# Twelve small VectorE instructions in place of a GpSimd power, and a 16x16 covariance in place of a pass of scores

## The chip, the cores and the metric

The kernel runs on one core of one Trainium2 chip. The core has a matrix engine (TensorE, PE in the profile, PEld its weight loads), a vector engine (VectorE, DVE), an activation engine (ScalarE, ACT), a general engine (GpSimd, POOL) and SyncE (SP), which issues most DMAs. Each engine runs its own instruction stream in order and waits on semaphores. The metric is the device time of one execution in microseconds; lower is better.

## The reference, cut to what matters

Sixteen batches (B = 16) of 512 queries of 256 numbers go through two transformer layers with a context of 1601 keys. In cut form:

```python
# layer 0, attention: 16 heads of 16; q and k are normalised per head
q = layernorm(q, ln_g, ln_b); k = layernorm(k, ln_g, ln_b)     # (x-mu)*rsqrt(var+1e-5)*g+b, over 16
attn = softmax(einsum('bhqd,bhkd->bhqk', q * 4, k)); out = attn @ v
x = x + out @ Wp + bp
x = x + gelu(LN(x) @ U1 @ V1 + b1) @ U2 @ V2 + b2              # layer 0, feed forward
# layer 1, attention: one head of 16 for all, scores normalised over the keys
q = LN(x) @ Wq + bq; k = ctx @ Wk + bk; v = ctx @ Wv + bv
s = einsum('bqd,bkd->bqk', q, k) / 16
s = (s - mean(s, -1)) / (std(s, -1, ddof=1) + 1e-8)
x = x + tile(softmax(s) @ v, 16) @ Wout + bout
# layer 1, feed forward: soft mixture of 64 experts (stage two of the kernel, untouched)
```

## The kernel before

The kernel has two stages with separate memory. Stage two (the experts, some 2230 us) is not touched. Stage one does both attentions and the first feed forward, batch after batch.

**Steps.** For one batch the heavy work of the first attention is cut into 4 groups of 4 heads x 13 chunks of keys = 52 steps. In a step c of a group the PE computes four blocks of scores (L766), which ACT exponentiates (L999), and multiplies the step before's probabilities with the values (L777, four matmuls). Between these stand up to six *row pieces*: scores of 401 keys for the group that comes next (L744), of which DVE takes the row maximum out of PSUM (L1148). The 64 pieces of a group are dealt as 6 in steps 0 to 8, 5 in steps 9 and 10, none in 11 and 12. The pieces go through two PSUM banks in turn, so the PE can be at most two pieces ahead of DVE. At the end of a group the maxima are transposed, split into three bf16 parts (`nT`, L1162 to L1166 on DVE) and written by DMA into a row of the query stack (`qst<-nT`, L532); the first score of the next group waits for it.

**The weave.** All other work is put between these by hand: `woven()` gives each small job a position, a step number with a fraction (thirds: three places in a step). Jobs with `of` = 1 are the *head* of the batch that comes next: load and transpose the context (`T`), keys and values (`K`), queries (`Q`), keys and values of the second attention (`kv1`), and the transposes of normalised heads (`X`). Jobs with -1 are the *tail* of the batch before: `attnT`, `proj`, the norms (`lnv`, `lna`), the feed forward (`xT`, `u1`, `V1`, `gpre`, `gtanh`, `gpost`, `U2`, `v2`) and the second attention (`q1`, `st` ... `out`). Each engine walks the same table and runs its own part of each job; an engine that waits inside a job holds back all that stands behind it. Before batch 0 the head runs alone, and after batch 15 the tail runs alone.

**Norm of heads.** POOL squares (`sq`, L591), DVE sums over 16 (`ssq`, L1142), and POOL in `kn` adds epsilon (L597), raises to the power -0.5 (L598) and multiplies (L600). This comes for five blocks n = 0 to 4 of a batch; block 1 is the queries, block 4 has 65 rows only. The PE's transposes `X` and then POOL's `X` (three instructions that split into bf16 planes, L607 to L609), the stores `stX` and the stack loads `ldS` of SP follow.

**Second attention.** `ldX` (SP) loads x and, by L519, the 32 x 1601 keys and values `kv1T`. `st` n is one of 16 passes of f32 scores, 128 queries x 401 keys (L845), read by DVE with bn_stats (L1211). `stv` joins them, `sgp` on POOL makes 1/(std + 1e-8) from the variance with two powers, `qtr` transposes the queries to tokens, `qs` scales them, `v1` transposes keys and values (L858), `qaT` transposes back, and `s1`, `pv1`, `o1`, `out` make scores, probabilities (ACT, L1044) and the output. The score's mean enters as a 17th row of the queries against a row of ones (`R1` = 65 partitions).

Of the kernel before, what the change touches and what calls it, by code (L numbers as in the profile page):

```python
# [59 lines left out]
def woven():  # L60
# [53 lines left out]
    for f in range(FC):  # L114
        put((10.67, 11.0, 11.34, 11.67, 15.67, 16.67, 17.67, 18.67)[f], -1, "V1", f)
        put((11.01, 11.5, 12.34, 13.0, 16.34, 17.34, 18.34, 19.34)[f], -1, "gpre", f)
        put((12.0, 12.67, 13.67, 14.34, 18.0, 19.0, 20.0, 21.0)[f], -1, "gtanh", f)
        put((12.01, 12.68, 13.68, 14.35, 18.01, 19.01, 20.01, 21.01)[f], -1, "gpost", f)
        put((15.34, 16.34, 17.34, 18.34, 20.0, 21.0, 22.0, 23.0)[f], -1, "U2", f)
# [157 lines left out]
def stage_one(nc, x, ctx_d, mask, w, x3_d, xn_d, xnT_d, ident, psum):  # L277

    with ExitStack() as st:
# [66 lines left out]
        kv1T = sb("kv1T", [R1, NK])  # L346
        v1a = sb("v1a", [P, KC, 2 * A1])
        q1T = sb("q1T", [R1, S])
        qa = sb("qa", [P, QT, R1])
        st1 = sb("st1", [P, QT, 4, 6])  # L350
        mv1 = sb("mv1", [P, QT, 2])
# [1381 lines left out]
```

## Time and profile before

| what | value |
|---|---|
| median of 3 runs | 7277.4 us (7277.04 to 7296.08) |
| the profiled execution | 7297.03 us, its span 7295.2 us |
| mean granted clock of TensorE | 0.952 |
| PE busy | 6573.1 us (90%) |
| PEld, DVE, ACT, POOL busy | 44%, 49%, 44%, 41% |
| head alone, up to the first score of batch 0 | to 258 us |
| 16 batches | last exponential starts at 4890.5 us; batch 10 takes 293.4 us |
| tail alone of the last batch | to 5068 us |
| stage two | to the end |

An engine's busy share is over the whole span. The granted clock is the rate of TensorE that the chip allowed, 1.0 being 2.4 GHz and 0.5 being 1.2 GHz. Step times below are the distances between the first exponentials of steps.

### The profile page before, as it was taken

To read this page: it belongs to the slowest core of one execution; us is meant where nothing else is said; L and a number is where in the kernel's file an instruction comes from. 1 tells how busy PE (TensorE), PEld (TensorE's weight loads), DVE (VectorE), ACT (ScalarE), POOL (GpSimd) and SP (SyncE) were. 2 spreads that over 40 slices of the span, in tenths; PEclk is the share of its full clock that TensorE was granted. 3 is DMA by queue.
4 is the path that set the end of the run, shared out by engine and by line. 5 is a ranking of instruction groups with operands and counts; after the bars stand their busy time and mean duration, and the time that the engine had idled before them with its cause. 6 is when DMAs were issued, how large, how long until landed. Compare 5 with 4: busy or idle time off the path is not lost. (4 is left out here: it accounts for less than half of the span.)

```text
span 7295.2 us, 92018 instructions
## 1 busy us (share of the span) xinstructions
PE 6573.1 (90%) x35805; PEld 3225.4 (44%) x35869; DVE 3609.2 (49%) x7012; ACT 3207.4 (44%) x5697; POOL 2959.5 (41%) x1969
## 2 busy tenths in 40 slices
PE   3789999999989999999999999985899999999999
PEld 1223333333333333333333333222788888766666
DVE  2555555655656556566565565641766666200000
ACT  1355555555555555555555555551322222111111
POOL 5327447365483663844736538223222222100000
PEclk8799999999999999999999999995999999999999
DMA  2341332432323323133242231302344444411111
GB/s 60 67 77 49 65 56 63 72 60 51 63 59 68 67 52 76 44 70 60 60 74 59 55 71 47 57 16 79 104 153 159 156 164 158 156 52 52 52 52 41
DMA packets 364931, 546.03 MB, mean 75 GB/s; under 512 B 59824, under 2 KB 281984, under 8 KB 364240
## 3 DMA queue, kind: packets, MB, share of 16 engines
q1 hardware_dynamic: 321232, 498.18, 28.2%
q10 hardware_dynamic: 43264, 41.95, 1.7%
q8 instruction: 284, 4.65, 0.3%
q14 instruction: 151, 1.24, 0.1%
HBM read 387.94 MB, written 151.28 MB: 74 GB/s over the span
## 5 line engine op out<-in xcount | busy, mean ns | idle before, releaser
L1148 DVE TENSOR_REDUCE mx<-psum 128x1 f32<-128x401 f32 x4096 | 2193.4, 570 | 1722.6 <-PE psum L744 1711.7
L999 ACT ACTIVATE probs<-psum 128x512 f32<-128x512 f32 (+1 forms) x3328 | 1920.1, 597 | 1149.4 <-PE psum L766 1145.8
L744 PE MATMUL psum<-kst,qst 96*128 96x401 bf16 x4096 | 1434.7, 352 | 268.3 <-DVE mx L1148 202.7
L766 PE MATMUL psum<-qst,kst 99*128 99x512 bf16 (+1 forms) x3328 | 1299.7, 394 | 152.1 <-ACT probs L999 116.6
L744 PEld LDWEIGHTS psum<-kst,qst 96*128 96x128 bf16 x4096 | 404.2, 99 | 1553.3 <-DVE mx L1148 1246.0
L777 PE MATMUL psum<-probs,vaug 128*17 128x512 f32 x6656 | 904.5, 616 | 0.0
L598 POOL TENSOR_TENSOR ssq<-ssq,powers 128x64 f32<-128x64 f32 (+1 forms) x80 | 722.2, 9027 | 6.7
L766 PEld LDWEIGHTS psum<-qst,kst 99*128 99x128 bf16 (+1 forms) x3328 | 330.9, 100 | 860.8 <-ACT probs L999 463.0
L1415 POOL TENSOR_TENSOR disp<-disp,rz 128x2048 f32<-128x2048 f32 x64 | 294.9, 4608 | 909.2 <-DVE rz L1634 909.2
L1434 PE MATMUL psum<-phi,xT 128*128 128x128 f32 x4096 | 511.7, 279 | 39.8 <-DMA xT<-xnT_scratch 32.5
L1434 PEld LDWEIGHTS psum<-phi,xT 128*128 128x128 f32 x4096 | 479.9, 193 | 87.4 <-issue 79.8
L1449 PE MATMUL psum<-disp,xnb 128*128 128x128 f32 x4096 | 489.3, 278 | 29.7 <-POOL disp L1415 19.0
L1585 ACT ACTIVATE disp<-psum 128x512 f32<-128x512 f32 x256 | 152.9, 597 | 807.7 <-PE psum L1502 606.2
L1512 PE MATMUL psum<-disp 128*128 128x257 f32 x2048 | 487.1, 381 | 12.3 <-issue 7.2
L1449 PEld LDWEIGHTS psum<-disp,xnb 128*128 128x128 f32 x4096 | 474.3, 194 | 37.9 <-POOL disp L1415 19.6
L1499 PE MATMUL psum<-xT,phi 128*128 128x512 f32 x1024 | 485.4, 596 | 0.2 <-issue 0.2
L1512 PEld LDWEIGHTS psum<-disp 128*128 128x128 f32 x2048 | 388.1, 190 | 143.5 <-issue 93.0
L625 POOL TENSOR_SCALAR rs<-mv 128x4 f32<-128x4 f32 x48 | 11.2, 232 | 1053.5 <-DVE mv L1204 1052.3
L702 PE MATMUL psum<-wkv,cT 128*128 128x512 f32 (+1 forms) x832 | 409.4, 615 | 14.0 <-ACT pl L992 6.3
L1536 ACT ACTIVATE disp<-psum 128x512 f32<-128x512 f32 x256 | 152.1, 597 | 463.1 <-PE psum L1434 463.1
L1687 DVE RECIPROCAL rc<-psum 128x1 f32<-128x1 f32 x64 | 5.8, 153 | 599.9 <-PE psum L1512 599.9
L1641 DVE TENSOR_TENSOR ysb<-psum,be 128x512 f32<-128x512 f32 x128 | 88.5, 692 | 428.9 <-PE psum L1464 428.9
(185 smaller groups left out, 7761.3 us busy)
## 6 DMA issues: line engine op xcount, KB each, us to landing
xnb<-xn_scratch SPq DMA_DIRECT2D x256, 512.0 KB, 3.7
kst<-k_planes SPq DMA_DIRECT2D x384, 200.1 KB, 9.1
k_planes<-pl SPq DMA_DIRECT2D x96, 384.0 KB, 3.2
y_scratch<-ysb ACTq DMA_DIRECT2D x128, 256.0 KB, 3.4
disp<-y_scratch SPq DMA_DIRECT2D x16, 2048.0 KB, 9.4
vaug<-v_scratch SPq DMA_DIRECT2D x64, 442.0 KB, 3.4
v_scratch<-vst SPq DMA_DIRECT2D x48, 544.0 KB, 3.1
cin<-in_ctx SPq DMA_DIRECT2D x48, 512.0 KB, 3.8
```

Source lines behind the costliest of these rows:

```text
L598: link(pool.tensor_tensor(r, r, powers[:, 0:1, None].broadcast_to((P, m, H)), ALU.pow))
L702: last = mm(hb[0:m, :], cT[:, n % 2, k, a * P:a * P + m], wkv[:, k, :], start=(k == 0), stop=(k == 1))
L744: mm(to[:, 0:PW], qst[g][0:NP, j, t * P:(t + 1) * P], kst[g][0:NP, j, k0:k0 + PW], start=True, stop=True).then_inc(m_full, 1)
L766: mm(bank[S_BANK[n % 2]][0:m, :], kst[g][0:NR, j, c * P:c * P + m], qst[g][0:NR, j, :], start=True, stop=True).then_inc(s_full, 1)
L777: last = mm(bank[V_BANK][32 * j:32 * j + HV, :], vaug[0:m, g % 2, c, HV * j:HV * (j + 1)], probs[0:m, 4 * (k % 2) + j, :], start=(c == 0), ...
L999: fn(probs[0:m, 4 * (k % 2) + j, :], bank[S_BANK[j % 2]][0:m, :], ACT.Exp, scale=float(HD) ** 0.5).then_inc(s_exp, 1)
L1148: v.tensor_reduce(mx[:, u // 4, u % 4:u % 4 + 1], bank[M_BANK[r % 2]][:, 0:PW], AX.X, ALU.max).then_inc(m_free, 1)
L1415: pool.tensor_tensor(d, d, rz[:, n % 2, None, :].broadcast_to((P, B, SL)), ALU.mult).then_inc(normed, 1)
L1434: last = mm(bank[u % 4][:, a * SL:(a + 1) * SL], xT[:, 4 * q + a, k, t * P:(t + 1) * P], phi[:, k, s * SL:(s + 1) * SL], start=(k == 0), s ...
L1449: last = mm(bank[4 + n % 2][:, (2 * a + h) * SL:(2 * a + h + 1) * SL], xnb[:, a, t, h * P:(h + 1) * P], disp[:, (QT * s + t) % RING, b, :] ...
L1499: mm(o, phi[:, k, c * P:(c + 1) * P], xT[:, b, k, :], start=(k == 0), stop=False)
L1512: last = mm(bank[4 + t][:, 0:D + 1], ex[n % 4][:, t * P:(t + 1) * P], ya[b % 2][:, e, :], start=(e == 0), stop=(e == NSL - 1))
```

## The change

**Inverse roots.** `kn` on POOL loses the add and the power. In their place `ssq` on DVE, behind its sum, makes the inverse root itself: an add, a shift and a multiply-add on the bits (a first guess from the constant `ROOT_SEED`), and three Newton steps of three instructions, twelve instructions, each waiting for the one before. They stand at 1.3 behind the block's last `K` or `Q` and not at 0.7.

**Variance from a covariance.** The 16 passes `st` and `stv`, `qtr` go. Since the variance of q.k over the keys is q' C q with C the covariance of the keys, DVE centres the keys at the start of the batch (`kc`: a sum over 1601, a scaling, a subtraction), PE transposes keys and values (`v1`, now at 1.67), multiplies keys by keys over 13 chunks (`cov`, 16x16), and DVE scales that (`cove`). Once the queries are there, PE makes C q (`cq`), DVE multiplies by q (`cqe`), PE sums over 16 and transposes (`cs`). With centred keys the row for the mean goes too, so operands shrink from 65 to 16 partitions.

**Places.** `attnT` moves from 3.34 to 4.0, some feed-forward jobs by a third of a step, and all of the second attention behind the queries moves 3 to 4 steps earlier: `s1` stands at 35.0, two a step, where it stood at 38.67, four in two steps; `st3`, the store of the tail, at 49.0 and not 51.67.

```diff
-        put(head[done] + 0.7, 1, "ssq", n)
-        put(head[done] + 0.72, 1, "kn", n)
+        put(head[done] + 1.3, 1, "ssq", n)
+        put(head[done] + 1.32, 1, "kn", n)
...
-    put(3.34, -1, "attnT", 0)
-    put(3.67, -1, "attnT", 1)
-    put(5.0, -1, "proj", 0)
+    put(4.0, -1, "attnT", 0)
+    put(4.34, -1, "attnT", 1)
+    put(5.34, -1, "proj", 0)
...
-    for n in range(16):
-        put(30.0 + n / 3, -1, "st", n)
-    put(35.67, -1, "stv")
-    put(35.7, -1, "sgp")
-    put(36.0, -1, "qtr")
-    put(36.67, -1, "qs")
-    put(37.0, -1, "v1")
-    put(37.34, -1, "qaT")
-    put(37.67, -1, "v1e")
-    put(38.0, -1, "q1a")
+    put(1.0, -1, "kc")
+    put(1.67, -1, "v1")
+    put(2.34, -1, "v1e")
+    put(3.0, -1, "cov")
+    put(3.5, -1, "cove")
+    put(30.0, -1, "cq")
+    put(30.67, -1, "cqe")
+    put(31.34, -1, "cs")
+    put(32.0, -1, "cse")
+    put(32.01, -1, "sgp")
+    put(33.0, -1, "qs")
+    put(33.67, -1, "qaT")
+    put(34.34, -1, "q1a")
     for c in range(KC):
-        put(38.67 + c // 4 * 2 + c % 4 / 3, -1, "s1", c)
+        put(35.0 + 0.5 * c, -1, "s1", c)
     for k in range(4):
-        put((40.34, 42.34, 44.34, 45.34)[k], -1, "pv1", k)
-    put(45.67, -1, "o1")
+        put((36.95, 38.95, 40.95, 41.95)[k], -1, "pv1", k)
+    put(42.34, -1, "o1")
...
-                r = ssq[:, n % 2, 0:m, :]
-                link(pool.tensor_scalar(r, r, HD * EPS, None, ALU.add))
-                link(pool.tensor_tensor(r, r, powers[:, 0:1, None].broadcast_to((P, m, H)), ALU.pow))
+                r = rstd[:, n % 2, 0:m, :]
...
             def heads_transposed(b, h):
                 pe.wait_ge(m_free, RING["out", b * G + G - 1] + 1)
-                if b >= 1:
-                    pe.wait_ge(t_act, at("t_act", b - 1, "xT", 3, h))
+                pe.wait_ge(t_dve, at("t_dve", b, "cove"))
...
+            def covariance(b):
+                pe.wait_ge(t_dve, at("t_dve", b, "v1e"))
+                for c in range(KC):
+                    m = key_rows(c)
+                    last = mm(b6[0:A1, 0:A1], kva[0:m, c, 0:A1], kva[0:m, c, 0:A1], start=(c == 0), stop=(c == KC - 1))
+                last.then_inc(t_mm, 1)
+
+            def covariance_queries(b):
+                pe.wait_ge(t_act, at("t_act", b, "q1"))
+                mm(b7[0:A1, :], cov[:, :], q1T[:, :], start=True, stop=True).then_inc(t_mm, 1)
...
-                v.tensor_reduce(ssq[:, n % 2, 0:m, :], sq[:, 0:m, :].rearrange("p c (h d) -> p c h d", h=H), AX.X,
-                                ALU.add).then_inc(ssq_done, 1)
+                z, y, t = ssq[:, 0:m, :], rstd[:, n % 2, 0:m, :], root[:, 0:m, :]
+                link(v.tensor_reduce(z, sq[:, 0:m, :].rearrange("p c (h d) -> p c h d", h=H), AX.X, ALU.add))
+                link(v.tensor_scalar(z, z, HD * EPS, None, ALU.add))
+                link(v.tensor_scalar(t.bitcast(I32), z.bitcast(I32), 1, None, ALU.logical_shift_right))
+                link(v.tensor_scalar(y.bitcast(I32), t.bitcast(I32), -1, ROOT_SEED, ALU.mult, ALU.add))
+                for i in range(3):
+                    link(v.scalar_tensor_tensor(out=t, in0=y, scalar=-0.5, in1=z, op0=ALU.mult, op1=ALU.mult))
+                    link(v.tensor_tensor(t, t, y, ALU.mult))
+                    ins = v.scalar_tensor_tensor(out=y, in0=t, scalar=1.5, in1=y, op0=ALU.add, op1=ALU.mult)
+                    if i < 2:
+                        link(ins)
+                ins.then_inc(ssq_done, 1)
...
+            def keys_centred(b):
+                dve.wait_ge(kv1_loaded, at("kv1_loaded", b, "ldX"))
+                link(v.tensor_reduce(kmean[:, :], kv1T[0:A1, :], AX.X, ALU.add))
+                link(v.tensor_scalar(kmean[:, :], kmean[:, :], 1.0 / NK, None, ALU.mult))
+                v.tensor_scalar(kv1T[0:A1, :], kv1T[0:A1, :], kmean[:, 0:1], None, ALU.subtract).then_inc(kc_ready, 1)
```

**POOL, block 4 of the head, steps 26 to 28 of the kernel before.** The inverse root of block 3 stands ahead of the squares of block 4, and between these and the root of block 4 stand a norm (`lna` 2) and a bias (`base` 3):

```order
L597 TENSOR_SCALAR ssq<-ssq 128x64
L598 TENSOR_TENSOR ssq<-ssq,powers 128x64
L600 TENSOR_TENSOR kraw<-kraw,ssq 128x1024
L591 TENSOR_TENSOR sq<-kraw 128x256
L625 TENSOR_SCALAR rs<-mv 128x4
L626 TENSOR_TENSOR rs<-rs,powers 128x4
L628 TENSOR_SCALAR xn<-xw,mv,rs 128x256 x4
L618 TENSOR_TENSOR xw<-xw,bor 128x1024
L597 TENSOR_SCALAR ssq<-ssq 128x16
L598 TENSOR_TENSOR ssq<-ssq,powers 128x16
L600 TENSOR_TENSOR kraw<-kraw,ssq 128x256
```

The same place in the changed kernel (the line numbers are its own):

```order
L607 TENSOR_TENSOR kraw<-kraw,rstd 128x1024
L600 TENSOR_TENSOR sq<-kraw 128x256
L632 TENSOR_SCALAR rs<-mv 128x4
L633 TENSOR_TENSOR rs<-rs,powers 128x4
L635 TENSOR_SCALAR xn<-xw,mv,rs 128x256 x4
L625 TENSOR_TENSOR xw<-xw,bor 128x1024
L607 TENSOR_TENSOR kraw<-kraw,rstd 128x256
```

The two powers are gone, and the norm and the bias still stand between the squares and the multiplication, so they run on POOL while DVE makes the root of block 4. In block 1 the three plane instructions of the first `X` stand in that place; in blocks 0, 2 and 3 the squares and the multiplication are neighbours.

**DVE, steps 1 to 3 of the changed kernel.** Before, there is nothing in these rows but maxima, `attn` and the moments of the queries:

```order
L1163 TENSOR_REDUCE mx<-psum 128x1 x7
L1224 TENSOR_REDUCE kmean<-kv1T 16x1
L1225 TENSOR_SCALAR kmean<-kmean 16x1
L1226 TENSOR_SCALAR kv1T<-kv1T,kmean 16x1601
L1163 TENSOR_REDUCE mx<-psum 128x1 x6
L1189 RECIPROCAL rec<-psum 128x16
L1191 TENSOR_TENSOR attn<-psum,rec 128x64 x4
L1138 BN_STATS bst<-cin 128x6 x4
L1141 BN_AGGR mv<-bst 128x2 x4
L1163 TENSOR_REDUCE mx<-psum 128x1 x2
L1252 COPY kva<-psum 128x12x32
L1253 COPY kva<-psum 65x32
```

The centring stands behind the seventh maximum of the batch (six of step 0 and one of step 1), and five maxima of step 1 stand behind it.

**PE, end of step 1 of the changed kernel,** with what each instruction waits for:

```order
L750 MATMUL psum<-kst,qst 128x401 [waits m_free]
L708 MATMUL psum<-wkv,cT 128x512 [waits h_free]
L708 MATMUL psum<-wkv,cT 128x512
L772 MATMUL psum<-qst,kst 128x512 [waits s_exp]
L750 MATMUL psum<-kst,qst 128x401 [waits m_free]
L847 MATMUL psum<-ident,kv1T 128x32 [waits t_act,kc_ready]
L847 MATMUL psum<-ident,kv1T 128x32 x11
L847 MATMUL psum<-ident,kv1T 65x32
L772 MATMUL psum<-qst,kst 128x512 [waits s_exp]
```

The transposes of keys and values, which stood in step 37, now stand ahead of the fourth score block of step 1 and wait for the centring.

## Rows read from the trace of the kernel before

**Rows 1.** The page's costliest groups: busy us, mean ns, idle before and its releaser.

```profile
L744 PE MATMUL psum<-kst,qst 96*128 96x401 bf16 x4096 | 1434.7, 352 | 268.3 <-DVE mx L1148 202.7
...
L598 POOL TENSOR_TENSOR ssq<-ssq,powers 128x64 f32<-128x64 f32 (+1 forms) x80 | 722.2, 9027 | 6.7
```

**Rows 2.** Stretches of batch 10: steps 1-3, 9, 12-15, 19-20, 27-28, 31-38, 39-45.

```profile
core 0: us, PE busy (x) PEld busy (x) DVE busy (x) ACT busy (x) POOL busy (x), PEclk, DMA share, GB/s
...
3195.40:3212.80 17.40, 16.23 (x80) 6.47 (x80) 11.93 (x32) 9.74 (x22) 8.48 (x7) 1.00 1.03 172
...
3242.90:3253.80 10.90, 7.62 (x35) 4.78 (x36) 5.06 (x8) 6.05 (x11) 9.47 (x3) 0.69 0.01 2
...
3266.30:3292.60 26.30, 23.65 (x95) 7.14 (x94) 11.28 (x24) 14.68 (x32) 23.68 (x22) 1.00 0.18 57
...
3311.00:3328.00 17.00, 13.83 (x47) 3.55 (x46) 6.37 (x13) 6.65 (x14) 15.90 (x17) 0.80 0.23 76
...
3360.40:3375.10 14.70, 10.92 (x61) 4.86 (x61) 8.55 (x20) 8.94 (x16) 14.09 (x12) 0.88 0.10 31
...
3385.50:3421.20 35.70, 34.39 (x184) 13.61 (x183) 27.19 (x62) 19.91 (x35) 3.73 (x7) 1.00 0.75 101
3421.20:3460.00 38.80, 37.40 (x182) 11.77 (x181) 23.23 (x47) 24.48 (x43) 0.00 (x0) 1.00 0.34 49
```

**Rows 3.** Timeline of steps 25 to 27 of batch 10: start, us, instruction, [idle before].

```profile
3349.15 10.56 POOL L598 TENSOR_TENSOR ssq<-ssq,powers 128x64 f32<-128x64 f32 x1
...
3361.68 0.61 POOL L591 TENSOR_TENSOR sq<-kraw 128x256 f32<-128x256 f32 x1
3362.33 0.42 DVE L1142 TENSOR_REDUCE ssq<-sq 128x16 f32<-128x256 f32 x1 [3.41 <-POOL sq L591]
...
3363.28 0.34 PE L744 MATMUL psum<-kst,qst 96*128 96x401 bf16 x1 [2.90 <-DVE mx L1148]
```

**Rows 4.** Timeline of step 19 of batch 10.

```profile
3316.16 0.63 ACT L1024 ACTIVATE gt<-gt 128x512 f32<-128x512 f32 x1 [4.62 <-POOL gt L640]
...
3317.34 0.61 PE L766 MATMUL psum<-qst,kst 99*128 99x512 bf16 x1 [2.90 <-ACT probs L999]
```

**Rows 5.** Groups by line and form, whole trace: a scores pass (two records each) and the sum.

```profile
L845 PE MATMUL psum<-kv1T,q1T 65*128 65x401 f32 x384 | 165.9, 517 | 0.9 <-ACT q1T L1032 0.9
...
L1142 DVE TENSOR_REDUCE ssq<-sq 128x64 f32<-128x1024 f32 x64 | 77.8, 1215 | 175.8 <-POOL sq L591 175.8
```

**Rows 6.** Steps 30 to 34 of batch 0, which has no tail woven in.

```profile
421.50:440.40 18.90, 17.50 (x94) 4.54 (x92) 15.48 (x31) 11.97 (x23) 1.16 (x3) 1.00 0.48 78
```

**Rows 7.** Timeline of the tail alone, from the first pass of scores to the first `s1`.

```profile
4986.86 20.00 PE L845 MATMUL psum<-kv1T,q1T 65*128 65x401 f32 x32 [0.86 <-ACT q1T L1032]
...
5011.15 0.23 DVE L1222 TENSOR_TENSOR qa<-psum,sg 128x64 f32<-128x64 f32 x1 [3.01 <-POOL sg L653]
...
5011.50 1.59 PE L858 MATMUL psum<-ident,kv1T 32*128 32x32 f32 x13 [3.37 <-DVE qa L1224]
...
5015.01 7.16 PE L878 MATMUL psum<-g_a,kv1T 65*128 65x512 f32 x8 [0.87 <-DVE g_a L1229]
```

**Rows 8.** All 64 of one DVE line that reads two SBUF operands: ns min/median/max.

```profile
L1166 DVE TENSOR_TENSOR nT<-nr,nT x64: 278/280/1269, 254.1 to 4838.5; 16x128 bf16<-16x128 f32 x64
```

**Rows 9.** The load of `kv1T`: its issue in batch 10, and its 16 landings.

```profile
3193.24 0.45 SPq L519 DMA_DIRECT2D kv1T<-kv_scratch  x1
...
DMA to landing us min/median/max: 4.8/7.2/10.3
```

**Rows 10.** The first score block of step 39, batches 10 and 7.

```profile
3420.78 0.39 PE L766 MATMUL psum<-qst,kst 99*128 99x512 bf16 x1 [0.39 <-DMA qst<-nT]
...
2532.57 0.61 PE L766 MATMUL psum<-qst,kst 99*128 99x512 bf16 x1 [3.02 <-DMA qst<-nT]
```

**Rows 11.** Timeline of the head alone: the power of block 0, and a transpose of block 3.

```profile
96.61 10.56 POOL L598 TENSOR_TENSOR ssq<-ssq,powers 128x64 f32<-128x64 f32 x1
...
182.81 1.08 PE L725 MATMUL psum<-ident,kraw 128*128 128x128 f32 x4 [9.96 <-POOL kraw L600]
```

More of the change, by code:

```diff
@@ L114, in woven @@
     for f in range(FC):
[L115 to L119, printed above, removed]
+        put((10.67, 11.0, 11.34, 11.67, 15.9, 16.67, 17.67, 18.67)[f], -1, "V1", f)
+        put((11.01, 11.5, 12.67, 13.67, 16.34, 17.34, 18.34, 19.34)[f], -1, "gpre", f)
+        put((12.34, 13.34, 14.0, 14.67, 18.0, 19.0, 20.0, 21.0)[f], -1, "gtanh", f)
+        put((12.35, 13.35, 14.01, 14.68, 18.01, 19.01, 20.01, 21.01)[f], -1, "gpost", f)
+        put((15.67, 16.34, 17.34, 18.34, 20.0, 21.0, 22.0, 23.0)[f], -1, "U2", f)
     put(23.67, -1, "pT2")
@@ L314, in stage_one @@
         sq = sb("sq", [P, 4, D])
-        ssq = sb("ssq", [P, 2, 4, H])
+        ssq = sb("ssq", [P, 4, H])
+        rstd = sb("rstd", [P, 2, 4, H])
+        root = sb("root", [P, 4, H])
         bst0 = sb("bst0", [P, QT, 6])
@@ L345, in stage_one @@
         gt = sb("gt", [P, S])
[L346 to L351, printed above, removed]
+        kv1T = sb("kv1T", [2 * A1, NK])
+        kva = sb("kva", [P, KC, 3 * A1])
+        kmean = sb("kmean", [A1, 1])
+        cov = sb("cov", [A1, A1])
+        q1T = sb("q1T", [A1, S])
+        qa = sb("qa", [P, QT, A1])
+        onec = sb("onec", [A1, 1])
+        qvar = sb("qvar", [P, QT])
         sg = sb("sg", [P, QT])
@@ L848, in queries_to_tokens, with layer_one_tokens @@
-            def queries_to_tokens(b):
-                pe.wait_ge(t_dve, at("t_dve", b, "st", 15))
-                for t in range(QT):
-                    last = tr(b6[:, t * A1:(t + 1) * A1], q1T[0:A1, t * P:(t + 1) * P], ident[0:A1, 0:A1])
-                last.then_inc(t_mm, 1)
-            def layer_one_values(b):
-                pe.wait_ge(t_dve, at("t_dve", b, "qs"))
+            def layer_one_tokens(b):
+                pe.wait_ge(kc_ready, at("kc_ready", b, "kc"))
+                if b >= 1:
+                    pe.wait_ge(t_act, at("t_act", b - 1, "xT", 3, 1))
@@ new lines, in covariance_queries, with score_variances @@
+            def covariance_queries(b):
+                pe.wait_ge(t_act, at("t_act", b, "q1"))
+                mm(b7[0:A1, :], cov[:, :], q1T[:, :], start=True, stop=True).then_inc(t_mm, 1)
+            def score_variances(b):
+                pe.wait_ge(t_dve, at("t_dve", b, "cqe"))
+                for t in range(QT):
+                    mm(b6[:, t:t + 1], cq[:, t * P:(t + 1) * P], onec[:, :], start=True, stop=True)
+                for t in range(QT):
+                    last = tr(b6[:, (t + 1) * A1:(t + 2) * A1], q1T[:, t * P:(t + 1) * P], ident[0:A1, 0:A1])
@@ L902, in _ @@
                      "attnT": heads_transposed, "proj": project, "xT": transpose_x, "u1": ffn_rank, "V1": ffn_up,
-                     "U2": ffn_down, "v2": ffn_out, "q1": layer_one_queries, "st": score_stats,
-                     "qtr": queries_to_tokens, "v1": layer_one_values, "qaT": scaled_queries, "s1": layer_one_scores,
+                     "U2": ffn_down, "v2": ffn_out, "q1": layer_one_queries, "v1": layer_one_tokens,
+                     "cov": covariance, "cq": covariance_queries, "cs": score_variances, "qaT": scaled_queries, "s1": layer_one_scores,
                      "pv1": layer_one_weigh, "out": layer_one_out}
@@ new lines, in covariance, with covariance_queries, score_variances @@
+            def covariance(b):
+                dve.wait_ge(t_mm, at("t_mm", b, "cov"))
+                v.tensor_scalar(cov[:, :], b6[0:A1, 0:A1], 1.0 / (NK - 1), None, ALU.mult).then_inc(t_dve, 1)
+            def covariance_queries(b):
+                dve.wait_ge(t_mm, at("t_mm", b, "cq"))
+                v.tensor_tensor(cq, b7[0:A1, :], q1T[:, :], ALU.mult).then_inc(t_dve, 1)
+            def score_variances(b):
+                dve.wait_ge(t_mm, at("t_mm", b, "cs"))
+                v.tensor_scalar(qvar[:, :], b6[:, 0:QT], 0.0, None, ALU.max).then_inc(sc_var, 1)
@@ L1233, in layer_one_values @@
                 bv = b6[:, 0:32 * KC].rearrange("p (c n) -> p c n", n=32)
[L1234 to L1238 removed]
+                v.tensor_copy(kva[:, 0:KC - 1, 0:2 * A1], bv[:, 0:KC - 1, :])
+                v.tensor_copy(kva[0:KL, KC - 1, 0:2 * A1], bv[0:KL, KC - 1, :]).then_inc(t_dve, 1)
+            steps = {"ln0v": first_moments, "ssq": square_sums, "res": residual, "lnv": moments, "kc": keys_centred, "cove": covariance,
+                     "cqe": covariance_queries, "cse": score_variances, "qs": scale_queries, "q1a": scaled_queries, "v1e": layer_one_values}
             alone(-1, steps)
```

85 lines of the change are left out of this document (28 added, 57 removed).

## Prediction

> **What bounds the kernel now.** I read the busy shares first, then the costliest groups, then one batch cut into stretches at its steps, then the timeline where a stretch is longer than its work. PE is busy 90% of the span, so stage one is a PE stream with holes. The groups [rows 1] name two things: the row pieces wait for DVE, 202.7 us in all, and one POOL line, the power, takes 722.2 us for 80 instructions, 10.6 us for one of 64 elements a partition. Whether that POOL time is on the path is not said by its sum but by the stretches [rows 2]. In most of them PE is busy nearly throughout; in four it is not: step 9 (7.62 of 10.90 us, mean granted clock 0.69), steps 12 to 15 (23.65 of 26.30), 19 and 20 (13.83 of 17.00, clock 0.80), 27 and 28 (10.92 of 14.70, clock 0.88). The timelines say why. In step 27 a power of 10.56 us holds the small squares behind it, DVE waits 3.41 us inside `ssq`, the maxima behind it on DVE are late, and PE is idle 2.90 us [rows 3]. In step 19 the gelu chain on POOL is late, ACT waits 4.62 us in `gtanh`, its exponential behind that is late, and PE is idle 2.90 us [rows 4]. So POOL is the bound in four places of a batch, PE elsewhere, and in steps 31 to 38 DMAs are near: the first score of step 39 waits 0.39 us for `nT` in batch 10 and 3.02 us in batch 7 [rows 10], since 24 loads of stacks, issued in steps 32 to 34, still drain ahead of it.
>
> **A, the powers gone from POOL.** For each of the four stretches I count its idle time above 0.3 us a step, and what the slow clock cost: (1 - clock) x length x busy share [rows 2]. Step 9: 3.28 - 0.3 + 0.31 x 10.9 x 0.70 = 5.4. Steps 12 to 15: 2.65 - 1.2 = 1.4. Steps 19, 20: 3.17 - 0.6 + 0.20 x 17.0 x 0.81 = 5.3. Steps 27, 28: 3.78 - 0.6 + 0.12 x 14.7 x 0.74 = 4.5. Together **-16.6 us a batch**, an upper bound.
>
> **B, twelve linked instructions on DVE.** No row of before has them. The nearest is a 128x64 product at 0.23 us [rows 7]; with the hand-over by semaphore I take 0.27, a chain of 3.2 us behind the sum of 1.2 [rows 5], so DVE is shut for 4.4 us; block 4 is smaller, some 2.5. PE is two pieces ahead at most; a DVE hole of 3.83 us (3.41 + 0.42) gave 2.90 us of PE idle [rows 3]. How much PE does meanwhile depends on the place: in step 5 both `proj` stand there (almost nothing lost, 0.8 with the crowded residuals of step 6), in step 16 less (1.5), in step 25 there are no pieces (0). In blocks 1 and 4 POOL is at work in that moment, as the order shows. The two-operand line L1166 takes 280 ns as a median but up to 1269 [rows 8]: nine of the twelve read two SBUF operands, so I add up to three POOL instructions there, and price step 9 at 2.5 and step 27 at 3.5. **+8.3 us a batch**; bounds 2 (all under PE work) and 17 (every hole passed on, with its slow clock).
>
> The Trainium skill, page "SBUF — State Buffer", section "Who interferes with whom", says that a VectorE instruction with two SBUF inputs and a GpSimd one that reads SBUF exclude each other for the whole instruction, whoever is first. The trace agrees, with the 1269 ns [rows 8]. If it bit in all blocks, the third rival below would be the outcome.
>
> **C, centring, transposes and covariance in steps 1 to 3.** The sum over 1601 elements costs 1.9 us by the 1215 ns of a sum over 1024 [rows 5], the subtraction between half of that and the same, together 3.1 to 4.0 us; I take 4.0. It first waits for `kv1T`. Its load is issued at 3193.24, 2.0 us into step 0 of batch 10, and takes 4.8 to 10.3 us, median 7.2 [rows 9], which is 5.0 us into step 1 (3195.4). `st3` is earlier now, so I expect the issue 3.5 us earlier and the landing 1.5 us into step 1; the centring ends at 5.5. PE reaches `v1` at about 3.4 in that step, ahead of the fourth score, and stands about 2.5 us, with 1.5 more for a clock that falls after such holes, as in the stretches of A [rows 2]. Behind that come 1.6 us of transposes (13 in 1.59 us [rows 7]) and `cov`, 26 short passes at the same 0.12, 3.2 us at most, 2.5 taken. Minus 0.6 of idle that those steps (17.40 us, 16.23 busy [rows 2]) have today: **+7.5 us a batch**; bounds 4 and 18.
>
> **D, the passes of scores gone.** A pass costs PE 0.86 us (165.9 us for 192 [rows 5]), 16 of them 13.8 us. In steps 31 to 38 (35.70 us [rows 2]) this buys little by itself: a bare step is 3.78 us anyway (five in 18.90 [rows 6]), and the stack loads with `nT` behind them take as long as now, so I leave that stretch at its length. But eight `s1` and two `pv1` move into it out of steps 39 to 45 (38.80 us [rows 2]), 8 x 0.86 + 2 x 1.0 = 8.9 us of PE work. Step 30 loses 0.9; 0.8 goes back where `pv1` now stands close behind the exponentials that it needs. **-9.0 us a batch**; bounds -5 and -12.
>
> **Ends.** In the head alone the power is in the chain: the 10.56 us of block 0 become 3.2, and PE's 9.96 us of waiting before block 3's transposes go [rows 11]. What is next late there is PE and ACT through one bank; I take 4 for block 0, 8 for block 3, and 4 for a store wait and block 4: **-16 us**. In the tail alone, first pass to first `s1` is 28.2 us (4986.86 to 5015.01 [rows 7]); the new chain (`cq` 1.8 at the half clock, product 0.7, `cs` 0.8, two powers and hand-overs 4.0, `qaT` 1.1, copy 0.7) is some 9, but centring, transposes and covariance, about 10 us, now stand ahead of `attnT`: **-9 us**. Batch 0 has A and B without C and D, and powers that also hold SP's queue back: -12. Batch 15 has C and D only: -1.5. Setup is behind the weights' loads: 0.
>
> **Sum.** -16.6 + 8.3 + 7.5 - 9.0 = -9.8 us a batch, times 14 = -137; with -12, -1.5, -16 and -9: -176 us. The profiled execution took 7297.0, so its like would take 7121; it stands 20 us above the median of the runs, against which I forecast 7277.4 - 176 = **7101 us**, -2.4%.
>
> **Rivals.**
> 1. *The DVE chains hide and the landing is early.* For it: DVE has only half its time in use. B falls to 2, C to 4: -16.6 + 2 + 4 - 9 = -19.6 a batch, and 7277.4 - 14 x 19.6 - 38 = 6965 us. Against it: the piece ring is two deep, and 2.90 us of idle followed from one DVE hole of 3.83 [rows 3].
> 2. *A late DMA takes the gain.* Either `kv1T` lands at its worst 10.3 us [rows 9], or steps 31 to 38 get shorter than the stack loads and each batch has batch 7's 3.02 us [rows 10] with several microseconds of half clock behind it. 9 us more a batch: -9.8 + 9 = -0.8, and 7277.4 - 11 - 38 = 7228 us. It decides at 12.5 us a batch (9.8 + 38/14). Against it: only some batches wait that long today.
> 3. *Slower: the shared port.* If POOL is at work in every chain, each of nine two-operand instructions waits for one POOL instruction of up to 1.27 us [rows 8], a chain of 3.2 us becomes about 13, and four of them add 4 x 9.8 = 39 us with what the clock loses: -9.8 + 39 = +29 a batch, 7277.4 + 14 x 29 - 38 = 7650 us. From a lengthening of about 3.1 us a chain on it decides the sign. Against it: in blocks 0, 2 and 3 POOL's multiplication stands next behind its squares, so POOL waits while DVE works.
>
> **How the numbers follow.** The forecast's own cases (7030 to 7215) get 0.66, the first rival 0.13, the second 0.13, the third 0.08. I split the second in three: 0.04 still faster, 0.05 within 0.3% (22 us, about what a measurement of this kernel can tell from no change), 0.04 slower. Faster: 0.66 + 0.13 + 0.04 = 0.83; same 0.05; slower 0.04 + 0.08 = 0.12. The range for eight in ten is 6985 to 7225: the third rival and most of the second's upper half lie outside, and a small part of the first.
>
> **What would show it.** Right: no power above 3 us on POOL in the head; step 9, 19 and 27 at 5 to 8 us; a chain of twelve DVE instructions of 2.5 to 3.5 us, 4 to 7 in blocks 1 and 4; PE standing 2 to 4 us ahead of `v1` in step 1; steps 31 to 38 still 35 to 36 us with PE at the end waiting for `nT`; steps 39 to 45 near 31. Wrong: a chain above 6 us in blocks 0 or 2, `v1` waiting over 6 us, or more slow clock in a batch than now.

## The result, and the profile after

The changed kernel takes 7435.8 us (median of 4 runs, 7429.5 to 7441.1) where the kernel before takes 7281.9 in the same comparison: a ratio of 1.0196, 95% interval 1.0177 to 1.0215. It is 2% slower; I had forecast 2.4% faster, and the time lies above my range. The profiled execution has a span of 7439.3 us and a mean granted clock of 0.925 (before 0.952).

From the page of the changed kernel, the clock row and the groups that answer to [rows 1]:

```profile
PEclk8899999899998999989999899885899999999999
...
L750 PE MATMUL psum<-kst,qst 96*128 96x401 bf16 x4096 | 1457.2, 357 | 360.1 <-DVE mx L1163 296.1
```

No power of the norm of heads is left on POOL, but the row pieces now wait 296.1 us for DVE against 202.7. The first and last exponential bound the woven batches (first and last start):

```profile
L1007 ACT ACTIVATE probs<-psum x3328: 569/597/657, 241.0 to 5045.8; 128x512 f32<-128x512 f32 x180, 65x512 f32<-65x512 f32 x16
```

The head ends at 241.0 us, where it ended at 258.2: -17.2. From the last exponential to the end it is 7439.3 - 5045.8 = 2393.5 us, where it was 7295.2 - 4890.5 = 2404.7: -11.2. In between lie 4804.8 us against 4632.3. So the whole loss, **+172.5 us**, is in the woven batches; I call this length, from first to last exponential, the *woven time* below. Batches 1 to 14, by their first exponentials, take 307.2 us each, all alike within 1 us. In the kernel before they average 296.0 and vary from 293 to 305; batch 10, which the stretches show, is one of the short ones (293.4), so its differences can't simply be multiplied by the number of batches.

Batch 10 of the changed kernel in stretches (steps 1-4, 9-10, 11-14, 15-16, 19-20, 27-29, 30-34, 35-38, 39-45, 46-51):

```profile
core 0: us, PE busy (x) PEld busy (x) DVE busy (x) ACT busy (x) POOL busy (x), PEclk, DMA share, GB/s
3262.80:3291.90 29.10, 26.92 (x144) 10.15 (x143) 18.73 (x44) 13.53 (x29) 8.47 (x8) 0.94 0.56 99
...
3317.10:3334.50 17.40, 13.70 (x61) 5.01 (x59) 11.09 (x25) 9.74 (x17) 8.80 (x8) 0.80 0.13 45
3334.50:3357.30 22.80, 21.67 (x88) 7.02 (x87) 8.18 (x16) 15.88 (x34) 17.30 (x18) 1.00 0.09 24
3357.30:3377.80 20.50, 16.84 (x57) 4.33 (x57) 11.23 (x31) 7.83 (x15) 11.70 (x10) 0.85 0.10 31
...
3390.10:3401.30 11.20, 10.92 (x47) 3.41 (x46) 6.33 (x13) 6.60 (x14) 9.86 (x10) 1.00 0.08 30
3433.70:3455.30 21.60, 16.58 (x83) 6.32 (x82) 15.75 (x37) 11.49 (x22) 13.24 (x12) 0.84 0.18 59
3455.30:3476.40 21.10, 19.87 (x111) 6.16 (x110) 16.75 (x35) 12.03 (x22) 3.46 (x6) 1.00 0.39 52
3476.40:3505.60 29.20, 28.84 (x93) 5.95 (x91) 7.05 (x16) 13.92 (x24) 0.00 (x0) 0.71 0.66 85
3505.60:3545.00 39.40, 36.39 (x159) 9.52 (x158) 26.80 (x63) 19.94 (x35) 2.58 (x4) 0.92 0.36 63
3545.00:3565.90 20.90, 19.32 (x105) 5.42 (x105) 12.96 (x28) 14.37 (x27) 3.53 (x3) 0.99 0.19 69
```

Two different things stand in these rows. Steps 9-10, 15-16 and 27-29 have idle PE and, with it, a lower clock: that is the pattern of [rows 2]. Steps 35-38 are of another kind: PE is busy 28.84 of 29.20 us, and yet the clock is 0.71. Not waiting but running slowly is what costs there. Cut where the clock falls, in steps 35 and 36:

```profile
3484.60:3491.80 7.20, 7.20 (x25) 1.10 (x24) 2.14 (x6) 2.37 (x4) 0.00 (x0) 0.55 1.04 122
3476.40:3484.60 8.20, 8.20 (x31) 2.19 (x30) 4.63 (x9) 5.20 (x9) 0.00 (x0) 0.97 1.10 137
```

and PE's timeline at that place:

```profile
3482.87 0.38 PE L772 MATMUL psum<-qst,kst 99*128 99x512 bf16 x1
3483.09 0.33 PE L750 MATMUL psum<-kst,qst 96*128 96x401 bf16 x1
3483.36 1.28 PE L886 MATMUL psum<-g_a,kv1T 16*128 16x512 f32 x2
3484.57 0.61 PE L772 MATMUL psum<-qst,kst 99*128 99x512 bf16 x1
3484.97 0.54 PE L750 MATMUL psum<-kst,qst 96*128 96x401 bf16 x1
```

PE had been busy 8.20 of 8.20 us when the clock went to its lower level (1.2 GHz); score and piece, 0.38 and 0.33 us, take 0.61 and 0.54 behind it. What PE did before the fall, and did not do in the kernel before, is `s1` with 16 rows (L886, `16*128`; 65 rows before). Whether that is the cause, the experiments have to say.

The holes of the chains are there too. Step 16, PE and DVE:

```profile
3366.84 1.21 DVE L1148 TENSOR_REDUCE ssq<-sq 128x64 f32<-128x1024 f32 x1
...
3370.85 0.23 DVE L1155 SCALAR_TENSOR_TENSOR rstd<-root,rstd 128x64 f32<-128x64 f32 x1
...
3371.62 0.52 PE L750 MATMUL psum<-kst,qst 96*128 96x401 bf16 x1 [2.49 <-DVE mx L1163]
```

DVE is shut from 3366.84 to 3371.08, 4.2 us; PE is idle 2.49 us and then runs at the lower level: the next two `V1` records take 2.07 us, against 1.12 in step 15.

### The profile page after: what moved, and what is told of

Read it like the earlier page. It is cut to its first block and busy times, and to the rows that moved or that the text cites. A ratio compares the mean times of both kernels' runs of the same rounds, so it can differ in the third digit from the quotient of the medians.

```text
span 7439.3 us, 92672 instructions
## 1 busy us (share of the span) xinstructions
PE 6715.5 (90%) x35869; PEld 3137.5 (42%) x35933; DVE 3783.8 (51%) x7729; ACT 3188.8 (43%) x5697; POOL 2206.5 (30%) x1793
## 5 line engine op out<-in xcount | busy, mean ns | idle before, releaser
L750 PE MATMUL psum<-kst,qst 96*128 96x401 bf16 x4096 | 1457.2, 357 | 360.1 <-DVE mx L1163 296.1
L772 PE MATMUL psum<-qst,kst 99*128 99x512 bf16 (+1 forms) x3328 | 1334.4, 405 | 71.0 <-ACT probs L1007 51.1
L783 PE MATMUL psum<-probs,vaug 128*17 128x512 f32 x6656 | 947.3, 644 | 0.0
L1467 PE MATMUL psum<-disp,xnb 128*128 128x128 f32 x4096 | 488.7, 277 | 30.2 <-POOL disp L1433 18.8
L886 PE MATMUL psum<-g_a,kv1T 16*128 16x512 f32 (+1 forms) x416 | 272.9, 744 | 0.9 <-DVE g_a L1247 0.9
```

What stands on the lines that cost most here:

```text
L750: mm(to[:, 0:PW], qst[g][0:NP, j, t * P:(t + 1) * P], kst[g][0:NP, j, k0:k0 + PW], start=True, stop=True).then_inc(m_full, 1)
L772: mm(bank[S_BANK[n % 2]][0:m, :], kst[g][0:NR, j, c * P:c * P + m], qst[g][0:NR, j, :], start=True, stop=True).then_inc(s_full, 1)
L783: last = mm(bank[V_BANK][32 * j:32 * j + HV, :], vaug[0:m, g % 2, c, HV * j:HV * (j + 1)], probs[0:m, 4 * (k % 2) + j, :], start=(c == 0), ...
L886: mm(to[0:m, :], kv1T[0:A1, c * P:c * P + m], q1a, start=True, stop=True).then_inc(signal, 1)
L1467: last = mm(bank[4 + n % 2][:, (2 * a + h) * SL:(2 * a + h + 1) * SL], xnb[:, a, t, h * P:(h + 1) * P], disp[:, (QT * s + t) % RING, b, :] ...
```

## The experiments

The kernel before was timed anew beside each group of kernels, and its medians differ (7281.9 with the result; 7309.7 beside kernels 1 to 4, 7290.4 beside 5 to 8, 7301.9 beside 9 to 11). So ratios are compared, and the woven time of each profiled execution (4632.3 before, 4804.8 after). A woven time is of one execution only; 13 executions of the kernel before, beside kernels 5 to 8, lay between 7259.7 and 7324.2 us. Where woven time and ratio differ, the ratio decides.

| kernel | median us | ratio to before (interval) | woven time against before |
|---|---|---|---|
| changed kernel | 7435.8 | 1.0196 (1.0177-1.0215) | +172.5 |
| 1: 65 rows in `s1` | 7242.2 | 0.9904 (0.9874-0.9935) | -26.6 |
| 2: before, 16 rows in `s1` | 7493.3 | 1.0248 (1.0216-1.0280) | +194.7 |
| 3: chains alone | 7321.0 | 1.0025 (1.0002-1.0047) | +38.1 |
| 4: covariance alone, 16 rows | 7449.5 | 1.0195 (1.0157-1.0233) | +159.4 |
| 5: 1 with the chain in four jobs | 7148.4 | 0.9794 (0.9764-0.9824) | -120.0 |
| 6: covariance alone, 65 rows | 7295.0 | 1.0003 (0.9985-1.0020) | +6.9 |
| 7: 32 rows in `s1` | 7362.6 | 1.0082 (1.0056-1.0109) | +97.2 |
| 8: 5 with the centring in two jobs | 7133.0 | 0.9774 (0.9748-0.9800) | -137.1 |
| 9: chains alone in four jobs | 7211.4 | 0.9859 (0.9811-0.9907) | -53.9 |
| 10: 8 with 128 rows in `s1` | 7121.4 | 0.9745 (0.9706-0.9784) | -123.6 |
| 11: 8 with the chain in five jobs | 7171.1 | 0.9813 (0.9780-0.9846) | -97.3 |

**1. The rows of `s1`, in the changed kernel.** My theory: the number of rows over which `s1` contracts pulls the clock down. Rival: the places do.

```diff
-        kv1T = sb("kv1T", [2 * A1, NK])
+        kv1T = sb("kv1T", [R1, NK])              # R1 = 65, zeros from row 32 on
...
-        qa = sb("qa", [P, QT, A1])
+        qa = sb("qa", [P, QT, R1])               # zeros from column 16 on
...
-        q1a = g_a[0:A1, :]
+        q1a = g_a[0:R1, :]
...
-                mm(to[0:m, :], kv1T[0:A1, c * P:c * P + m], q1a, start=True, stop=True).then_inc(signal, 1)
+                mm(to[0:m, :], kv1T[:, c * P:c * P + m], q1a, start=True, stop=True).then_inc(signal, 1)
```

> The changed kernel with one thing put back: the 13 score matmuls s1 contract over 65 partitions again (rows 32 to 64 of the keys and 16 to 64 of the queries are zeros), instead of 16. Places, chains, covariance stay. Theory R (rows): TensorE falls to half clock in steps 36 to 40 of the changed kernel although PE is busy without a gap, because a 16-row f32 matmul counts as little activity; with 65 rows the clock stays full there, steps 36, 38 and 40 (9.2, 9.7 and 8.5 us) fall to 5.2, 6 and 6, some 9 to 10 us a batch: about 7295 us, half-clock time of the span down from 1124 to about 820 us. Rival P (places): the clock falls because of where the jobs stand and of holes before; then 65 rows change under 15 us: 7420 to 7450.

7242.2 us, ratio 0.9904. Its steps 35-38 and 39-45 of batch 10:

```profile
3355.90:3376.50 20.60, 19.13 (x93) 6.15 (x92) 7.01 (x16) 13.75 (x25) 0.00 (x0) 1.00 0.80 111
3376.50:3411.70 35.20, 32.10 (x159) 9.86 (x157) 26.58 (x63) 19.91 (x35) 1.33 (x3) 1.00 0.40 73
```

The same 93 and 159 records at the same places, the clock at 1.00, and 8.6 and 4.2 us less. The added rows of the queries hold zeros, so every added product is zero, and still the clock is another. The rival of places falls. The gain was larger than I expected (2.9% of the kernel before, against some 140 us).

**2. The rows of `s1`, in the kernel before.** The opposite way round, with all instructions and places of before; the kernel leaves out the score's mean.

```diff
-                mm(to[0:m, :], kv1T[:, c * P:c * P + m], q1a, start=True, stop=True).then_inc(signal, 1)
+                mm(to[0:m, :], kv1T[0:A1, c * P:c * P + m], q1a[0:A1, :], start=True, stop=True).then_inc(signal, 1)
```

> The kernel before with one thing changed: its s1 matmuls contract over rows 0 to 15 only (the score's mean is left out, which the softmax does not see; the variance and all else stay). Instructions and places are those of before. Theory R: half clock appears in steps 39 to 45, where before has none, and a batch gets 5 to 9 us longer: 7282 + 15 x 7 = about 7390 us. Rival P: only the 0.05 us that a 16-row pass takes longer, 13 x 0.05 x 15 = 10 us: about 7292.

7493.3 us, ratio 1.0248: some 180 us, where I had put 105 on it. Steps 39-45, which answer to the last row of [rows 2], and the group of `s1`:

```profile
3534.20:3589.60 55.40, 54.61 (x181) 11.87 (x181) 23.48 (x47) 24.57 (x42) 0.00 (x0) 0.72 0.24 34
...
L878 PE MATMUL psum<-g_a,kv1T 16*128 16x512 f32 x384 | 269.7, 793 | 0.9 <-DVE g_a L1229 0.9
```

38.80 us at 1.00 have become 55.40 us at 0.72, with PE busy 54.61 of them. The account closes to 0.2 us: 13 `s1` at 0.10 us more each (two records take 1.12 us with 16 rows at full clock, 1.02 with 65) are 1.3 us, the clock (1 - 0.72) x 55.4 = 15.5, together 38.8 + 16.8 = 55.6, against 55.4 measured.

**3. The chains alone.** The kernel before with the inverse roots of the changed one and their places, nothing else.

> The kernel before with the inverse roots on VectorE at their new places, and nothing of the covariance. My terms A and B said -8.3 us a batch and some -28 at the ends: 7140. Theory H (holes), from the changed kernel's steps: 9 and 10 together 17.4 us as before, 15 and 16 20.5 against 14.2, 19 and 20 11.2 against 15.7, 27 to 29 21.5 against 20.9, so the holes of the chains and the half clock behind them give back what the powers gave: +1 to +3 us a batch, 7270 to 7310 us.

7321.0 us, ratio 1.0025, which is some 7300 us beside the result's 7281.9: what theory H said, and not the -8.3 us a batch of A and B. Steps 15-16 of its batch 10, 18.8 us where before has 14.3 (3284.6 to 3298.9):

```profile
3291.50:3310.30 18.80, 15.15 (x57) 4.07 (x57) 11.16 (x31) 7.81 (x14) 7.89 (x7) 0.94 0.09 29
```

This kernel's batch 10 is level with that of before (293.5 against 293.4 us); the average of batches 1 to 14 is 298.3 against 296.0. Most of its loss stands in other batches than the one shown.

**4. The covariance alone, with 16 rows.** The changed kernel with add and power back on POOL, at +0.7.

> The changed kernel with the inverse roots back on GpSimd at the places of before; covariance, places of the second attention and 16 rows stay. If R holds, most of the loss is here: after - 16 for the head + about 0 to -3 us a batch for the chains: 7400 to 7450 us. If the loss lay with the chains: 7150 to 7250. My terms C and D alone said 7282 - 21 - 9 = about 7250.

7449.5 us, ratio 1.0195, at the upper edge of what theory R gave: a loss as large as that of the changed kernel is there without the chains.

**5. The chain in four jobs.** Kernel 1, the twelve instructions dealt over four thirds of steps.

```diff
-        put(head[done] + 1.3, 1, "ssq", n)
-        put(head[done] + 1.32, 1, "kn", n)
+        put(head[done] + 1.3, 1, "sum", n)       # sum, add, shift, multiply-add
+        put(head[done] + 1.64, 1, "nr", n, 0)    # a Newton step, three instructions
+        put(head[done] + 1.97, 1, "nr", n, 1)
+        put(head[done] + 2.3, 1, "ssq", n)       # the third, signals POOL
+        put(head[done] + 2.32, 1, "kn", n)
```

> The changed kernel with 65 rows in s1, and the chain of twelve cut into four jobs (sum and first guess at +1.3, then one Newton step of three instructions at +1.64, +1.97 and +2.3), so that row maxima stand between; the number of DVE instructions is the same. Theory H (hole): PE loses time only because DVE is shut in one piece; steps 15 and 16 fall from 20.3 back to 14.5 to 15.5 us, the clock does not drop there, 5 to 7 us a batch in all: about 7150 us. Rival L (load): the chain's 3 us of DVE work is what costs, wherever it stands: under 1 us a batch, 7225 to 7250.

7148.4 us, ratio 0.9794, as theory H said. No DVE work was taken away, so the rival of load falls. (The multiplication on POOL comes a step later with it; what that alone is worth was not run.) Steps 15-16 and 27-29 of batch 10, and DVE where the hole was (step 16):

```profile
3167.30:3182.80 15.50, 14.05 (x56) 3.68 (x55) 10.48 (x26) 7.78 (x14) 10.40 (x10) 1.00 0.12 40
...
3240.10:3258.70 18.60, 14.91 (x83) 5.29 (x82) 15.16 (x37) 11.56 (x22) 14.25 (x13) 1.00 0.20 68
```

```profile
3178.57 0.20 DVE L1157 TENSOR_SCALAR rstd<-root 128x64 int32<-128x64 int32 x1
3178.80 1.06 DVE L1173 TENSOR_REDUCE mx<-psum 128x1 f32<-128x401 f32 x2
3179.78 0.21 DVE L1162 SCALAR_TENSOR_TENSOR root<-rstd,ssq 128x64 f32<-128x64 f32 x1
```

Two maxima stand between the first guess and the first Newton step, and the clock stays at 1.00 in steps 9-10, 15-16 and 27-29, where it was 0.90, 0.86 and 0.84 in kernel 1. A part comes back in steps 30-34, 22.7 us at 0.92 (kernel 1: 21.2 at 1.00). Over the whole trace the row pieces wait some 47 us less for DVE than in kernel 1 (L751 there, L754 here):

```profile
L751 PE MATMUL psum<-kst,qst 96*128 96x401 bf16 x4096 | 1440.5, 353 | 362.0 <-DVE mx L1166 299.7
...
L754 PE MATMUL psum<-kst,qst 96*128 96x401 bf16 x4096 | 1425.3, 349 | 317.2 <-DVE mx L1173 252.5
```

**6. The covariance alone, with 65 rows.**

> Covariance alone with 65 rows in s1, the inverse roots on GpSimd. If the rows cost the same here as in the changed kernel (194 us): 7449 - 194 = about 7255 us, a batch near 290. Then C and D with their places are worth some -30 us against before; my terms gave 7250. If the rows' cost came only with the chains of Newton: 7400 or more.

7295.0 us, ratio 1.0003: with the rows put right, C and D and their places are worth nothing by themselves, where I had some -30 us. The rows cost 1.9% here (kernel 4 against this one), 2.9% with the chains (changed kernel against kernel 1). Its steps 1-4 are 31.5 us and its steps 35-38 20.5:

```profile
3192.10:3223.60 31.50, 28.30 (x144) 10.76 (x143) 19.98 (x45) 13.50 (x29) 11.45 (x10) 0.89 0.57 97
...
3408.40:3428.90 20.50, 19.03 (x92) 6.05 (x91) 6.98 (x16) 13.68 (x24) 0.00 (x0) 1.00 0.91 114
```

**7. 32 rows.** Kernel 1 with 32 rows.

> The changed kernel with s1 over 32 rows (16 of them zeros in the queries). If a 32-row matmul costs the clock as little as one of 65 rows: 7240. If it is like 16 rows: 7430. If the number of rows counts in proportion, between the two, nearer to 16 rows: 7350 to 7400.

7362.6 us, ratio 1.0082: between the two, nearer to 16 rows. Steps 36-38 of batch 10 are 22.7 us at 0.71 (16 rows: 24.0 at 0.64; 65 rows: 16.1 at 1.00):

```profile
3436.40:3459.10 22.70, 21.96 (x71) 4.49 (x70) 4.05 (x10) 10.50 (x19) 0.00 (x0) 0.71 0.60 79
```

This bears on a rival that kernels 1 and 2 leave standing: that it is the longer pass, with the gap before its weight load, and not the number of rows that pulls the clock down. Two records of `s1` take 1.12 us at full clock with 32 rows, as with 16, and 1.02 with 65:

```profile
3438.18 1.12 PE L887 MATMUL psum<-g_a,kv1T 32*128 32x512 f32 x2
```

Between 16 and 32 rows the pass is as long, and 1.1% lies between the kernels all the same; so the longer pass is not the whole cause. Between 32 and 65 rows both change together, and no run parts them.

**8. The centring in two jobs.**

```diff
-    put(1.0, -1, "kc")
-    put(1.67, -1, "v1")
...
+    put(1.0, -1, "kcs")                          # the sum over 1601
+    put(1.67, -1, "kc")                          # scaling, subtraction
+    put(2.34, -1, "v1")                          # v1e 2.67, cov 3.34, cove 3.67
...
-    put(6.34, -1, "res", 1, 0)
+    put(6.0, -1, "res", 1, 0)
```

> As the first kernel of this call, and the centring cut into two jobs as well (sum at 1.0, scaling and subtraction at 1.67, transposes and covariance a third to two thirds later), with the first residual back at 6.0. By theory H step 1 falls from 8.9 to some 6.5 us and steps 7 and 8 from 13.4 to 11.5: 3 to 5 us a batch below the first kernel, about 7090 us. By L no change against it.

7133.0 us, ratio 0.9774: less gain than expected (about 7090 us), and the intervals of kernels 5 and 8 overlap, so the split of the centring is not shown to be worth anything. In batch 10 its steps 1-4 take 28.2 us (kernel 5: 27.9) and steps 5-8 25.1 (26.4): PE is idle 1.35 us in steps 1-4 and not 2.45, but the clock there is 0.94 and not 1.00. Steps 27-29 are longer, 20.5 us at 0.83 against 18.6 at 1.00.

**9. The chains alone, in four jobs.**

> The kernel before with the inverse roots on VectorE in four jobs (as in the split kernel), and nothing of the covariance. The one-piece version took 7321 us. If the holes of the chains were all that spoiled it, the split gives here what it gave with the covariance, some 94 us: about 7227 us, 0.7 to 1% below before; then the split kernel's 7148 owes some 80 us to the covariance, its places and 65 rows. If the covariance is worth nothing with 65 rows (covariance alone was level with before): about 7150 us here.

7211.4 us, ratio 0.9859. In woven time the split is worth 92 us here (from +38.1 to -53.9) and 93 with the covariance (from -26.6 to -120.0). That these agree so well is luck: by the ratios it is 1.7% here and 1.1% there. But it is clear of the noise in both, so it is a property of the chains, and the 66 us of woven time between kernels 9 and 5 belong to the covariance and its places (both have 65 rows).

**10. 128 rows.**

> The fastest kernel so far (7133 us: chain in four jobs, centring in two, 65 rows) with s1 over 128 rows, the added ones zeros. From 16, 32 and 65 rows the time went 7436, 7363, 7242 us; if the clock still gained from rows, 7100 or less; if 65 rows are enough for the clock in these steps, as steps 36 to 41 at full clock with 65 rows say, the same within 15 us: 7120 to 7150.

7121.4 us, ratio 0.9745, within the 7120 to 7150 of "65 rows are enough". Its interval overlaps that of kernel 8: no difference that these runs can tell.

**11. The chain in five jobs.** Kernel 8 with the sum at +1.0 and the first guess by itself at +1.34.

> The fastest kernel so far with the chain in five jobs: the sum of 1.2 us at +1.0, the first guess at +1.34, the Newton steps as they are. By the theory of holes the longest piece shrinks from 2.0 to 1.2 us, which the two-deep ring of pieces may cover: steps 5 and 6 (14.5 us) and 17 and 18 (13.7) lose up to 1 us each, 7100 to 7125. If four jobs were enough, or the earlier sum waits for the squares: 7130 to 7160.

7171.1 us, ratio 0.9813: outside both ranges. It is not faster than kernel 8; the intervals of the two just overlap, so that it is slower is not quite shown (batches 1 to 14 average 289.1 us in its profile, 286.1 in that of kernel 8). I did not follow up why.

## Why the prediction was wrong, by its own steps

**The step that is missing.** The forecast priced the shrinking of the operands from 65 to 16 partitions at nothing: D counts `s1` at 0.86 us wherever it stands. It costs 199 us of woven time (kernel 1 to the changed kernel), 195 in the kernel before (kernel 2) and 152 without the chains (kernel 6 to 4): 9.5 to 13 us a batch. In the stretches it comes nearly all through the granted clock. To mend this step alone is enough to turn the sign: with 65 rows (kernel 1) the changed kernel is 1.0% faster than before. Why few rows pull the clock down no run shows. I had even named "more slow clock in a batch than now" as a sign of being wrong, but looked for its cause only in holes.

**A, the powers gone.** Right in kind. Steps 19-20 went from 17.1 to 11.2 us at a clock of 1.00 (A: -5.3), steps 11-14 from 24.3 to 22.8 (A: -1.4). In steps 9-10 and 27-29 the gain can't be seen by itself, since the chain stands there; with the chain dealt out (kernel 5) they are 3.6 and 1.5 us shorter than before (A: -5.4 and -4.5), so A's sum was indeed an upper bound.

**B, the chains.** Their length was right: with the sum ahead 4.2 us in step 16 (forecast 4.4); in block 1, where POOL is at work, 5.7 with the sum and 4.5 without (forecast 4 to 7); in block 4 5.3 without. The sum of block 1, its first Newton instruction and its last:

```profile
3319.29 1.21 DVE L1148 TENSOR_REDUCE ssq<-sq 128x64 f32<-128x1024 f32 x1
...
3321.88 1.06 DVE L1153 SCALAR_TENSOR_TENSOR root<-rstd,ssq 128x64 f32<-128x64 f32 x1
...
3324.79 0.23 DVE L1155 SCALAR_TENSOR_TENSOR rstd<-root,rstd 128x64 f32<-128x64 f32 x1
```

What failed is the price of a hole. In batch 10 of kernel 3, against before, steps 5-8 are +1.3 us, 9-10 -0.7, 15-16 +4.5, 17-18 +0.5, 27-29 +1.6. With A taken as forecast, which is its upper bound, the chains cost 1.3, -0.7 + 5.4 = 4.7, 5.0 and 1.6 + 4.5 = 6.1: 17.1 us, not 8.3. That is about my own upper bound of 17 ("every hole passed on, with its slow clock"); with less gain in A it would be less. I had let PE's other work cover the hole, in step 5 nearly all of it and in step 16 in part; but in step 16 of the changed kernel PE has done that work by 3369.13 and then stands 2.49 us all the same, and the stretch at half clock behind it costs about as much as the stand (0.15 of 20.5 us, at a busy share of 0.82: 2.5 us). Over batches 1 to 14 kernel 3 averages +2.3 us a batch where A and B were to give -8.3, so the two together are off by 10.6; in woven time they were to give -128 us (14 x 8.3 + 12), and kernel 3 gives +38.1. Kernels 5 and 9 show that the fault lies in the one piece, not in the twelve instructions.

**C, centring to covariance.** Steps 1-4 take 29.1 us against 24.4, +4.7, where C said +7.5 with a lower bound of 4 (kernel 6, with the powers on POOL, has 31.5, +7.1). The landing was in time: the centring starts 0.75 us into step 1 and ends at 3.8 (forecast 1.5 and 5.5). The stand ahead of `v1` that C priced at 2.5 us did not come: over the whole trace `v1` waits 4.0 us for the centring, all in one place. In batch 10 PE stands 1.17 us at the row piece ahead of it instead, since the maxima queue behind the centring:

```profile
3267.14 0.34 PE L750 MATMUL psum<-kst,qst 96*128 96x401 bf16 x1 [1.17 <-DVE mx L1163]
```

The sum took 1.80 us and the subtraction 1.04 (forecast 4.0 for both):

```profile
L1224 DVE TENSOR_REDUCE kmean<-kv1T 16x1 f32<-16x1601 f32 x16 | 28.8, 1798 | 0.0
L1226 DVE TENSOR_SCALAR kv1T<-kv1T,kmean 16x1601 f32<-16x1601 f32 x16 | 16.7, 1044 | 0.6
L847 PE MATMUL psum<-ident,kv1T 32*128 32x32 f32 x192 | 15.9, 232 | 4.0 <-DVE kv1T L1226 4.0
```

Not in the sum at all were steps 5-8: 25.2 us against 23.2, with or without the chains (kernel 6 has 25.2 too). There `attnT`, `proj` and `res` stand a third to two thirds of a step later and closer together, which I take for the reason; kernel 8 moves one `res` back, among other things, and its steps 5-8 take 25.1.

**D, the passes of scores gone.** With 65 rows (kernel 1, batch 10 against before) steps 30-34 are -4.0 us, 35-38 +5.1, 39-45 -3.6, 46-51 -3.8: -6.3, within the bounds of -5 to -12 but short of -9.0. I expected steps 31-38 to keep their length behind the stack loads; in fact they got shorter first (30-34) and longer then, since what moves in is more PE work than what moves out (PE is busy 19.13 us in steps 35-38, 14.19 before). Steps 39-45 gave 3.6 us and not 8.9, as later jobs of the second attention came forward into them; their gain stands in steps 46-51, which D left out. And 0.86 us is a pass over 401 keys [rows 5]; one `s1`, of 512 columns, takes 1.02 with 65 rows at full clock. In the changed kernel, at half clock, the same four stretches are -4.1, +13.7, +0.6 and -3.7: +6.5.

**C and D with their places** were to give -23 us of woven time and gave +6.9 (kernel 6). Chains and covariance together with 65 rows give -26.6, where the two alone add up to +45.0 (38.1 + 6.9). These 72 us (1.2% by the ratios) come of the two together and stay open in the main. Batch 10 shows where its part lies (-3.3 us). With the powers left on POOL, kernel 6 has 36.6 us at a clock of 0.91 in steps 21-26, where the kernel before, kernel 3 and kernel 1 all have 32.4: the chains give these 4.2 us back. On the other side, kernel 6 has 13.4 us in steps 9-10 and 14.4 in 19-20 with its powers still there (17.4 and 17.1 before), so the new places alone give part of what A counted as its own. With 16 rows the two do not add up in the same way: 38.1 + 159.4 against 172.5, 25 us. The account of the woven time against the forecast of -150.7 is then 199 for the rows, 166 for A and B, 30 for C and D, minus 72: 323, which is 172.5 + 150.7.

**Ends.** Head -17.2 (forecast -16) and the end -11.2 (forecast -9) were right. Batch 0 has A and B without C and D, and shared their fault: from 258.2 to 513.4 it took 255.2 us, now, from 241.0 to 494.5, 253.5, so -1.7 and not -12.

**The rivals.** Neither of the first two came: the chains do not hide (only the early landing of that rival did come), and no DMA is late (PE waits 13.7 us for `nT` in the whole trace, in two places). The third had the right sign and the wrong mechanism: a chain with POOL at work is lengthened by 1.5 us in block 1 and by some 2.8 in block 4 (5.3 us, against an estimated 2.5 for twelve instructions of 0.17 us with their hand-overs), not by 10. In block 1 part of it falls on instructions with one SBUF operand, which I had not counted: the add and the shift took 0.40 and 0.64 us there, 0.20 each in step 16. A chain lengthened by 3.1 us was to turn the sign; what turned it was the rows, which none of the rivals had.

## What to carry to other kernels

Where PE is the bound, count what a change does to the granted clock as well as to the work: fewer rows in a matmul took no time off a pass and cost this kernel 1.9 to 2.9%, and padding them with zeros gave it back. A chain of dependent small instructions on the engine that feeds PE belongs between that engine's short jobs, not in one piece; the same twelve instructions cost up to 17 us a batch in one piece, and dealing them out gave back 1.1 to 1.7% of the kernel, some 6 us a batch. Undo one part of a change at a time before believing a sum of terms: here two faults and one sound idea stood in one diff, and the versions with both mended (kernels 5, 8 and 10) are 2.1 to 2.6% faster than the kernel before.
